# Products of the identity that nobody reads, in TensorE's waits in the tail and ahead of attention's first scores

## What is computed

```python
xn = _layernorm(x)
# layer 0: 8 heads of 8 on each half of the features, the second half smoothed over time
x1 = layernorm(xh + mha(xh, ...)); x2 = layernorm(xsh + mha(xsh, ...))
y = concatenate([x1, x2], -1)
s = layernorm(y + relu(y @ w_ff1.T + b_ff1) @ w_ff2.T + b_ff2)
g = silu(moe(xn))            # 32 experts, 4 per token, capacity 640, and a shared one
x = x + s * g
# layer 1: a selective scan on one side, a feed-forward with routed weights on the other
xn = _layernorm(x)
x = x + mamba(xn) * silu(routed_ffn(xn))
```

## Time and profile before

| | us |
|---|---|
| median of 3 executions | 1946.66 |
| lowest, highest | 1943.94, 1963.69 |
| the profiled execution, its own time | 1945.57 |
| its span in the trace | 1943.8 |
| granted clock of TensorE, mean | 0.958 of full speed |
| TensorE busy | 1734.7 (89%) |
| VectorE busy | 1641.7 (84%) |
| ScalarE busy | 1519.3 (78%) |

### The profile page before, as it was taken

The page is one execution under the profiler, slowest core; times in us unless marked ns, Lnnn a source line. Parts: engine busy times, 40 slices in busy tenths (PEclk is TensorE's granted clock), DMA queues, the critical chain, the costliest instruction groups (busy, mean ns, idle before and its releaser), DMA issues.

```text
span 1943.8 us, 41195 instructions
## 1 busy us (share of the span) xinstructions
PE 1734.7 (89%) x15427; PEld 669.0 (34%) x15428; DVE 1641.7 (84%) x2488; ACT 1519.3 (78%) x2881; POOL 521.7 (27%) x795
## 2 busy tenths in 40 slices
PE   6799999999999999999999999999953667799884
PEld 4322222222222222222222222248821333366553
DVE  7799999999999999999999999915443656499778
ACT  6579999999999999999999999973312556877565
POOL 2432300320002222322232231000055653033425
PEclk9899999999999999999999999999976888899897
DMA  4423221210111111111111111038752432332121
GB/s 121 160 67 103 66 64 54 83 42 26 29 43 37 44 55 43 42 53 46 41 50 51 41 59 32 13 97 233 212 153 58 115 107 75 112 90 58 36 71 44
DMA packets 151356, 142.14 MB, mean 73 GB/s; under 512 B 38986, under 2 KB 130125, under 8 KB 151010
## 3 DMA queue, kind: packets, MB, share of 16 engines
q1 hardware_dynamic: 142818, 122.36, 21.5%
q0 software_dynamic: 8352, 17.29, 3.2%
HBM read 76.60 MB, written 60.03 MB: 70 GB/s over the span
## 4 chain that ended last, share of the span: by engine, by line
PE 67%; DVE 11%; ACT 11%; issue 5%; another core or an unknown queue 3%; DMA 2%; SPq 1%; POOL 0%; ACTq 0%; DVEq 0%; POOLq 0%
PE PS L1909 27%; PE PS L1937 16%; PE PS L1893 10%; ACT probs L1279 6%; PE PS L1987 3%; PE PS L1972 2%; DVE hst L1041 1%; PE PS L1964 1%; PE PS L2099 1%; DVE VP L1018 1%; DVE VP L1026 1%; DVE YM L924 1%; PE PS L2036 1%; PE PS L2029 1%
## 5 line engine op out<-in xcount | busy, mean ns | idle before, releaser
L829 DVE TENSOR_REDUCE mxp<-PS 128x1 f32<-128x1024 f32 x1024 | 1171.8, 1213 | 24.1 <-PE PS L1893 18.0
L1279 ACT ACTIVATE probs<-PS 128x512 f32<-128x512 f32 x2048 | 1094.8, 598 | 63.7 <-PE PS L1937 20.1
L1909 PE MATMUL PS<-probs,VH 128*32 128x256 f32 x8192 | 642.2, 391 | 1.8 <-ACT probs L1279 0.6
L1937 PE MATMUL PS<-stacks 51*128 51x512 bf16 x2048 | 440.3, 387 | 19.5 <-ACT probs L1279 16.9
L1893 PE MATMUL PS<-stacks 48*128 48x512 bf16 x2048 | 418.2, 380 | 10.0 <-DMA stacks<-qkl_d 8.8
L1909 PEld LDWEIGHTS PS<-probs,VH 128*32 128x32 f32 x8192 | 173.0, 108 | 413.2 <-issue 235.5
L1937 PEld LDWEIGHTS PS<-stacks 51*128 51x128 bf16 x2048 | 116.3, 93 | 459.7 <-ACT probs L1279 406.8
L1749 POOL DMA_INDIRECT VP<-oe_d,ROWI x128 | 130.9, 1022 | 236.9 <-DMA oe_d<-stacks 159.1
L1639 POOL DMA_INDIRECT xe_d<-xn_s,rows_s x128 | 126.3, 987 | 217.0 <-PE PS L1909 175.6
L1617 POOL CAST spl<-nmx 128x8 bf16<-128x8 f32 x64 | 12.0, 188 | 506.2 <-DVE nmx L824 296.6
L1893 PEld LDWEIGHTS PS<-stacks 48*128 48x128 bf16 x2048 | 105.7, 95 | 25.3 <-DVE mxp L829 12.3
(11 more groups left out here) (363 smaller groups left out, 1857.2 us busy)
## 6 DMA issues: line engine op xcount, KB each, us to landing
stacks<-qkl_d SPq DMA_DIRECT2D x128, 96.0 KB
xe_d<-zt SPq DMA_DIRECT2D x16, 640.0 KB
stacks<-xe_d SPq DMA_DIRECT2D x32, 320.0 KB, 3.8
oe_d<-stacks SPq DMA_DIRECT2D x32, 320.0 KB, 3.3
stacks<-qkl_d SPq DMA_DIRECT2D x128, 64.0 KB
o_d<-SG SPq DMA_DIRECT2D x256, 32.0 KB
ews<-in_ew_dram SPq DMA_DIRECT2D x33, 192.0 KB, 2.5
stacks<-qkl_d SPq DMA_DIRECT2D x128, 32.0 KB
```

The costliest lines, as they stand in the source:

```text
L829: v.tensor_reduce(mxp[:, n // 2, n % 2:n % 2 + 1], MXB[n % 2].rearrange("p a c -> p (a c)"), X_AX, ALU.max).then_inc(mx_done, 1)
L1279: act.activation(probs[:, at:at + 512], PS[:, bank_of(u, e), :], ACT.Exp, scale=float(1.0 / np.sqrt(np.float32(DK)))).then_inc(exp_done, 1)
L1909: mm = pe.matmul(OB[32 * jg:32 * jg + 32, c:c + 256], VH[w][:, kt, :], probs[:, at:at + 256], start=(kt < 2 and half == 0), stop=(kt >= TC ...
L1937: pe.matmul(PS[:, bank_of(u, e), :], KS[w][o:o + KROWS + 3, kt * P:(kt + 1) * P], QS[w][o:o + KROWS + 3, q0:q0 + 512], start=True, stop=Tr ...
```

## The change

Ahead of the wait for `qk_ld`, `max_chunk(0)` now waits for `rest` and then issues 13 products of the identity with four copies of the identity, 128 x 512 in fp32, into bank 4. In the tail a new helper `stay_busy(n)` issues n of them into bank 2. It stands ahead of the loop (7), ahead of turn_y(0) at s = -1 (10), ahead of turn_y(1) at s = 0 (8), ahead of turn_ff(1) at s = 1 (12) and ahead of turn_ff(s) at s = 2 to 6 (5 each). Nothing waits for these products and nothing reads them; TensorE's stream, being one queue, runs through them. Nothing is removed.

```diff
 def max_chunk(m):
     u, n = divmod(m, CHUNKS)
+    if m == 0:
+        pe.wait_ge(rest, NB - 1)
+        for _ in range(13):
+            pe.matmul(tiles4(MXB[0][:, 0, :]), ident[:, :], ident[:, :].unsqueeze(1).broadcast_to([P, TB, P]), start=True, stop=True)
     if n == 0:
         pe.wait_ge(qk_ld[u % 4], 192 * (u // 4 + 1) + (32 if u % 4 else 16))
...
+def stay_busy(products):
+    for _ in range(products):
+        pe.matmul(tiles4(PS[:, 2, :]), ident[:, :], ident[:, :].unsqueeze(1).broadcast_to([P, TB, P]), start=True, stop=True)
+
 pe.wait_ge(sg_done, E)
 pe.wait_ge(oe_out, E)
+stay_busy(7)
 for s in range(-2, NB):
...
     if s >= 0:
+        if 0 < s < NB - 1:
+            stay_busy(12 if s == 1 else 5)
         turn_ff(s)
     if 0 <= s + 1 < NB:
+        if s <= 0:
+            stay_busy(10 if s < 0 else 8)
         turn_y(s + 1)
```

## The result

| | before | with the products |
|---|---|---|
| median, us | 1950.39 (4 executions) | 1979.87 (4 executions) |
| lowest to highest | 1943.94 to 1963.69 | 1972.87 to 1984.68 |
| the profiled execution | 1945.57 | 1972.87 |

The ratio is 1.0135, interval 1.0101 to 1.017: the change costs 29.5 us. Forecast were 1955 and a range up to 1972.

What follows compares the result with a forecast made beforehand. The tail was taken as bound by a chain of short steps between four engines, with late releases absorbing TensorE's delays. Terms 0 + 0 + 1.5 + 1.4 - 1.1 + 0 + 1 + 2 + 4.3 = +9.1 gave 1955 us, range 1937 to 1972.

Steps and rivals of the forecast that it cites:

- the cover: Early tail: late releases, 19.7 us at turn_y(1), absorb what products ahead of turn_y(0) and turn_y(1) overrun; failing, up to +9.7.
- Price of a product, the clock, ahead of attention: 0.86 us per product at full clock; 13 ahead of attention keep PEclk 1.00 from 65 to 84, net 0.
- Ahead of the loop, 7, and ahead of turn_y(0), 10: Start of tail: the 7 sum to 0; the 10 put turn_y(0) 2.8 late, counted in a joint +1.5 with turn_y(1)'s 8.
- Ahead of turn_y(1), 8: At s = 0: 6.9 us, held by the 19.7 late release; +1.5 together with the 10 ahead of turn_y(0).
- 12 at s = 1: Ahead of turn_ff(1): 6.5 late, 2.7 back from the clock, combine(2) loses its 2.37 late release; +1.4.
- 5 at s = 2: Ahead of turn_ff(2): 4.3 us fit into a 6.41 wait and the clock gives some back; -1.1.
- 5 at s = 3 to 6: Ahead of turn_ff(s), no wait, each delays the chain by 4.3; taken as 0, +1, +2, +4.3, bounds 0 and 17.2.
- Rival 2: Tail: handovers slip into the slow part of a gather burst, 16 on top of 9, 1971 us; chance 0.14.
- Rival 1: Tail: the chain hides the products' overruns and the clock is paid back; -0.7, 1941 to 1949 us; chance 0.26.
- Rival 3: A gain through the clock, 22 us, faster than the forecast range; chance 0.05.
- Rival 4: A loss beyond the slow end of the range, tested by the price of a product; chance 0.03.

Runs made afterwards that it cites:

- e1: Only the 13 products ahead of attention added to the kernel before; 1891.24 us against 1890.8 beside it, ratio 1.0003.
- p2: The changed kernel with all products, its gathers replaced by plain copies from SP's queue; 1891.97 us, kernel before beside it 1890.19.
- p1: The kernel before, no products, its gathers replaced by plain copies from SP's queue; 1866.3 us against 1890.19.
- p6: Plain copies in place of the gathers, with products cut to fit TensorE's waits (10, 4, 5, 7, 3); 1863.71 us, kernel before beside it 1890.73.
- f2: Real gathers with products cut to fit TensorE's waits, timed once more; 1949.8 us against 1946.48 for the kernel before, ratio 1.0025.
- b_again: The kernel before, unchanged, run once more for a trace; 1890.31 us, with 1890.19 beside it.
- a_again: The changed kernel with all products, run once more; 1890.98 us against 1890.19 for the kernel before, ratio 1.0007.
- f: Real gathers with products cut to fit TensorE's waits, against the kernel before; 1887.16 us against 1890.97, ratio 0.998.

## Why the prediction was wrong

It said +9.1 us; measured were +29.5 where the late releases are, 0 where the gathers set the pace, and +25.5 to +25.7 where there are no gathers. The step that failed is the cover: the late releases, waits whose release the profile doesn't show, were taken as waits of fixed end and length, which swallow what TensorE does in them. In the trace of the changed kernel they are neither at the same places nor as long as before, 92 us of the chain instead of 64; and without the gathers, where no such wait is left, the blocks cost 22.3 us in the steps and not 9. How the 29.5 us are shared between the products' own price and the growth of the late releases stays open.

- **Price of a product, the clock, ahead of attention.** Right: 0.865 us; PEclk 1.00 from 65 to 79; third pair of scores as before, once the 1.44 are taken off; 1.0003 in e1.
- **Ahead of the loop, 7, and ahead of turn_y(0), 10.** Right as 0 for the 7, in the forecast's own condition too: turn_residual(0) (L2020) comes 2.7 later than before (1430.64 against 1427.94), and the tail itself began 2.6 later. For both blocks p2 says the same: its combine(0) starts at 1441.90, p1's at 1441.88; among p1 to p6 this start scatters from 1440.44 to 1443.33. With the late releases combine(0) starts at 1451.78 and not at 1447.38, and has two waits named remote of 4.5 each inside.
- **Ahead of turn_y(1), 8.** I found their 6.9 us of length and then let the late release of 19.7 hold them, for +1.5 with the 10. "If turn_ff(0) still comes at 1457.05" was the condition, and it failed: it came at 1482.41. The 19.7 on ScalarE's L1336 is gone, and 14.9 and 11.7 on VectorE are there. These 8 are not on the chain after; a late release of 12.15 is, at the same place. Where no late release covers them they cost 6.8 (p2).
- **12 at s = 1.** +1.4 forecast. TensorE's shift was right, 6.3 us against 6.5. What failed is that I took off the late release of combine(2), 2.37: all 10.3 us of the block are on the chain after, late releases of 2.46 and 4.21 stand on it behind them, and the step from combine(1) to combine(2) grew by 5.1 (21.46 to 26.51). With the gathers off they stand in a longer wait, 6.43, and the +1.6 of p2 are another sum, which says nothing of this one.
- **5 at s = 2.** -1.1 forecast, -0.7 in p2's step. Right there; they are not on the chain of the changed kernel.
- **5 at s = 3 to 6.** I had read that TensorE didn't wait and that each block delays the chain by 4.3, and then took 0, +1, +2, +4.3. Without gathers 3.4, 3.4, 3.4 and 4.3 are measured (p2), 14.5 in all, and there the bound of 17.2 was nearer than the value taken from inside it. In the trace of the changed kernel those of s = 5 and 6 are on the chain, 4.34 each, and those of s = 3 and 4 aren't, so in the forecast's own condition this term isn't shown to be far off.
- **Block by block, in the forecast's own condition.** The starts of the eight combines lie 4.4, 8.1, 13.2, 25.8, 16.7, 21.8, 15.4 and 24.4 us behind those of the trace before. The loss goes up and down by 10 us where blocks of equal length stand, so no price of a block can be read from these two traces.
- **Rival 2** had the size (+25) and the side. That the handovers slip and the late releases grow is what the chain shows (64 to 92 us). Against it as the whole cause stands that without any gathers the price is 25.5 to 25.7 too, by another sum. Between that and 29.5 lie 4 us, less than the scatter of four executions (1972.87 to 1984.68). f2 shows that such a sum can differ by 12 us at nearly the same time. It is neither shown nor refuted, and what the late releases are is open.
- **Rival 1** (the chain hides the overruns) is what happens under the other condition, through the gathers' pace and not through late releases. I had not seen it as a case, because in the trace before the gathers pause for 13.09 us. In b_again, without late releases, that pause is missing, so I take them to have made it.
- **Rival 3** is refuted by the time, and a_again shows that its mechanism isn't there: in it the tail is at 0.99 of full clock and no faster, the clock was no bound. Its 22 us were too many in any case: at s = 3 to 6 the transposes of L2042 take 0.60 and not 1.12, so these steps were at full clock already.
- **Rival 4** is refuted by the price of 0.865.

The rule of the Trainium skill (TensorE: Matmul & The Clock Gate, "Why this matters for your kernels": keep the gaps between bursts of matmuls short) agrees with the rows on the clock, and a_again shows what it doesn't say: a warm clock is worth what the chain gets of it. In p6 that is 3.7 us of the steps; f gains 3.8 us under one condition, and f2 nothing under the other.

## What to carry to other kernels

Products that keep the clock up are free only up to the wait that they fill, and that wait has to be read at each place of the stream: the same count in every step of a loop costs its length wherever the engine came just in time. Ask of an idle engine whether its wait is on the chain; where another queue sets the pace (here GpSimd's gathers, 1.30 us each), neither the products nor the clock they save move the end. And don't let a wait whose release the profile doesn't show absorb a term of the sum: its end is not fixed. Here turn_ff(0) stood behind such a wait at 1457.05 in one trace and at 1482.41 in the other. Time the kernel before again beside every experiment: the same change cost 29.5 us on one occasion and nothing on another.

## What the runs showed of the hardware

The same kernel took 1946 us in some runs and 1891 in others, with a mean granted clock of 0.99 up to 1420 us in the traces of both. The difference arises in the tail: VectorE's first combine starts at 1446.33 in b_again and at 1447.38 in the profile of before, its last addition to x (L934) at 1611.86 and at 1671.12. In between, only the profile of before has waits on ScalarE and VectorE for a release that no instruction shows, up to 19.7 us for one. With the gathers replaced by copies from SP's queue the two conditions came within 3 us of each other (1866.3 and 1869.5). So these releases are seen only with the indirect DMAs on GpSimd; what delays them, and why only in some runs, is open.
